# A decoder kernel on one core: table load, two preparations, one copy and six identity turns moved or cut in the sparse attention stage

## The chip, the core and the metric

The kernel runs on one core of a Trainium2 chip. A core has a matrix engine (TensorE, PE in the profile), a vector engine (VectorE, DVE), an activation engine (ScalarE, ACT), a general engine (GpSimd, POOL) and a queue engine (SyncE, SP). Each follows its own list of instructions, and they meet only at semaphores. The metric is the device time of one execution in microseconds (us), less is better.

## The reference, cut to what matters

The reference is a decoder of two layers over 8 sequences of 256 tokens, width 128. The first layer is a recurrent attention, a memory attention and a mixture of experts with one expert each token; the second a sparse attention, a cross attention and a mixture with two experts each token. The change is in the sparse attention only:

```
def _sparse_causal_mask(q_len, k_len):
    cols = np.arange(k_len)
    rows = np.arange(k_len)[:, None]
    strided = cols % STRIDE >= STRIDE - C          # STRIDE 128, C 8
    local = cols[None, :] // STRIDE == rows // STRIDE
    causal = cols[None, :] <= rows
    layout = (strided[None, :] | local) & causal
...
q, k, v = (split(q), split(k), split(v))           # 16 heads of 8
scores = jnp.einsum('bhqd,bhkd->bhqk', q, k) * scale
scores = jnp.where(mask, scores, mask_value)
attn = jax.nn.softmax(scores, axis=-1)
out = jnp.einsum('bhqk,bhkd->bhqd', attn, v)
out = out.transpose(0, 2, 1, 3).reshape(B, S, E)
return out @ W_proj + b_proj
```

A query in the first 128 tokens of a sequence sees the keys of its own tile of 128 up to itself. One in the second 128 sees, besides those, the last 8 keys of the first tile; these are called the far keys.

## The kernel before

The 8 sequences go through in 4 groups of 2, that is 512 tokens or 4 tiles of 128 each time. Every group passes the stages memory, first mixture, sparse attention, cross attention, second mixture, one after the other; the recurrent part of the next group is done beside the later stages. The order of work on each engine is written out by hand, and semaphores join the engines. ScalarE's program runs the first three groups as a loop and the last one after it.

In the sparse stage the scores of 16 heads are cut into 8 units. Unit u is eight heads of one tile (128 queries by 8 times 128 keys); the tiles go in the order 0, 1, 3, 2, two units each, so units 2 to 5 belong to tiles that have far keys. A unit passes these steps:

- `masked_scores(u)` on TensorE: the causal mask is laid into two PSUM banks (L868), and the scores are added (L880). From u = 2 on it waits for `s_arg`, since the banks of unit u - 2 must have been read.
- `unit(u)` on VectorE: the negative row maximum (L2113), for units with far keys its minimum with that of the far scores, `far_nmax` (L2116), then scores plus maximum into an SBUF buffer (L2120), which counts `s_arg` up.
- `exps(u)` on ScalarE: the exponential of that buffer (L1423), which counts `s_exp` up.
- `turn_probs(u)` on TensorE: 16 transposes into PSUM banks 4 and 5 (L893). It waits for `s_exp` and for `sT_ready`, that the turned probabilities of unit u - 1 were copied out of these banks.
- `turned(u)` on ScalarE: that copy (L1239, 128x1024), which counts `sT_ready` up.
- `values(n)` on TensorE for each tile, after both its units (L920, L925).

For the far keys there are apart from this a score for each sequence (L860), a copy of these scores by ScalarE (L1239, 128x256, which counts `far_ready` up), and on VectorE two preparations: `Vg`, the far values under the head mask (L2166), and `far_nmax` (L2170). `far_exps(b)` (L1437) is their exponential on ScalarE, `turn_far` (L900) their transpose.

An exponential and a Gelu are in different function tables of ScalarE. The first mixture ends with a Gelu, so a table is loaded ahead of the first exponential of the sparse stage. `keep_awake(5, n)` (L494) is n transposes of the identity into an unused part of bank 5; nobody reads the result. `decay_e` is a column of 128 that is read once, before the first group; the memory stage already computes it again at its start.

Of the kernel before, what the change touches and what calls it, by code (L numbers as in the profile page):

```python
# [9 lines left out]
ACT = mybir.ActivationFunctionType  # L10
# [30 lines left out]
R_LNG, R_LNB, R_FLNG, R_FLNB, R_DECAY, R_FIRST, R_MK, R_MV, R_MR, R_FMK, R_FMR, R_NORMW = range(12)  # L41
# [21 lines left out]
def decoder_kernel(  # L63
# [10 lines left out]
    with ExitStack() as stack:  # L74
        def sb(name, shape, dt=F32):
            return stack.enter_context(nc.sbuf_tensor(name, shape, dt))
# [27 lines left out]
        decay_e = sb("decay_e", [P, 1])  # L104
# [187 lines left out]
        def bank(i):  # L292
            return ps[:, i, :]

        def far_turn(n):
            return ps[:, 7, 2 * P:3 * P] if n == 1 else ps[:, 0, 0:P]
# [115 lines left out]
        def col(i):  # L412
            return cols[:, i:i + 1]
# [76 lines left out]
        def _(pe):  # L490
            def keep_awake(b, count):

                for _ in range(count):
                    pe.transpose(ps[:, b, 2 * P:3 * P], ident[:, :], ident[:, :])  # L494
# [343 lines left out]
            def sparse_attention(it):  # L838
# [45 lines left out]
                def turn_probs(u):  # L884
                    pe.wait_ge(s_exp, it * UNITS + u + 1)
                    if u:
                        pe.wait_ge(sT_ready, it * UNITS + u)
                    else:
                        pe.wait_ge(far_ready, it + 1)
                    for i in range(2 * QUAD):  # L890
                        for w in range(2):
                            r = slice(w * DK, (w + 1) * DK)
                            last = pe.transpose(ps[:, 4 + w, i * DK:(i + 1) * DK], SP_[u % 2][r, i, :], ident[r, r])  # L893
                    last.then_inc(sT_ps, 1)
# [43 lines left out]
                def masked_scores(u):  # L938
                    mask_scores(u)
                    scores(u)  # L940
# [2 lines left out]
                masked_scores(1)  # L943
                far_scores_of()
                masked_scores(2)
                keep_awake(5, 5)
                turn_probs(0)
                masked_scores(3)
                turn_probs(1)
# [272 lines left out]
            def group(it, more=True):  # L1222
                memory(it)
                mixture_top1(it)
                sparse_attention(it)
                cross_attention(it, more)
                mixture_top2(it, more)
# [9 lines left out]
        def _(act):  # L1237
            def copy(dst, src):
                return act.activation(dst, src, ACT.Copy)  # L1239
# [19 lines left out]
            def x_turned(it, n):  # L1259
                for seq in range(GROUP):  # L1260
                    act.wait_ge(xT_ps, (it * LAYERS + n - 1) * GROUP + seq + 1)
                    r = slice(seq * SEQ, (seq + 1) * SEQ)
                    copy(XT[:, r], ps[:, XT_BANKS[n - 1][seq], r]).then_inc(xT_ready, 1)
# [76 lines left out]
            def context_values(it, j, b, seq):  # L1340
                act.wait_ge(vx_ps, it * (2 * PAIRS) + V_ORDER.index((j, seq)) + 1)
                copy(values_of(j, seq), tiles(b)).then_inc(vx_ready, 1)
# [68 lines left out]
            def sparse_attention(it):  # L1411
                act.wait_ge(cols_ready, 6)
                x_turned(it, 3)
                context_values(it, 3, 6, 0)
                act.wait_ge(qkv_ps, it * 4 + 1)
                act.activation(qT[:, :], bank(1), ACT.Identity, bias=battq_scaled[:, 0:1], scale=float(HD) ** -0.5)\
                    .then_inc(qk_ready, 1)
                act.wait_ge(qkv_ps, it * 4 + 2)
                act.activation(kT[:, :], bank(2), ACT.Identity, bias=col(R_BATT + 1)).then_inc(qk_ready, 1)

                def exps(u):
                    act.wait_ge(s_arg, it * UNITS + u + 1)
                    act.activation(SP_[u % 2], SP_[u % 2], ACT.Exp).then_inc(s_exp, 1)  # L1423

                def turned(u):
                    act.wait_ge(sT_ps, it * UNITS + u + 1)
                    if u in (3, 4):
                        act.wait_ge(so_ps, it * TT + 1)
                    if u == 5:
                        act.wait_ge(s_ps, it * UNITS + UNITS)  # L1430
                    if u in (6, 7):
                        act.wait_ge(so_ps, it * TT + 2)
                    copy(sp_turned[u], ps[:, 4:6, :].rearrange("p b n -> p (b n)")).then_inc(sT_ready, 1)

                def far_exps(b):
                    act.wait_ge(g_arg, it * GROUP + b + 1)
                    act.activation(G[:, b, :], G[:, b, :], ACT.Exp).then_inc(g_exp, 1)  # L1437

                def far_turned(b):
                    act.wait_ge(gT_ps, it * GROUP + b + 1)  # L1440
                    copy(GT[:, b, :], far_turn(SP_ORDER.index(b * QT + 1))).then_inc(gT_ready, 1)

                act.wait_ge(far_ps, it + 1)
                copy(far_scores, ps[:, 4, 0:GROUP * P].rearrange("p (b n) -> p b n", b=GROUP)).then_inc(far_ready, 1)
                exps(0)
                turned(0)
                exps(1)
                turned(1)
                exps(2)
                exps(3)  # L1450
                far_exps(0)
                turned(2)
                exps(4)
                turned(3)
                far_turned(0)
                exps(5)
                far_exps(1)
                turned(4)
                turned(5)
                exps(6)  # L1460
                exps(7)
                turned(6)
                far_turned(1)
                turned(7)
                context_values(it, 2, 3, 1)
# [115 lines left out]
            def group(it, more=True):  # L1581
                memory(it)
                mixture_top1(it)
                sparse_attention(it)
                cross_attention(it, more)
                mixture_top2(it, more)
# [225 lines left out]
        def _(dve):  # L1812
# [293 lines left out]
            def sparse_attention(it):  # L2106
                def unit(u):
                    n, w = u // 2, u % 2
                    t = SP_ORDER[n]
                    nm = s_nmax[:, n, w * 2 * QUAD:(w + 1) * 2 * QUAD]  # L2110
                    scored = ps[:, 2 * w:2 * w + 2, :].rearrange("p b (i k) -> p (b i) k", k=P)
                    dve.wait_ge(s_ps, it * UNITS + u + 1)
                    dve.tensor_reduce(nm, scored, AX.X, ALU.max, negate=True)  # L2113
                    dve.drain()
                    if t % QT == 1:
                        dve.tensor_tensor(nm, nm, far_nmax[:, t // QT, w * 2 * QUAD:(w + 1) * 2 * QUAD], ALU.min)  # L2116
                        dve.drain()
                    if u >= 2:
                        dve.wait_ge(sT_ps, it * UNITS + u - 1)
                    dve.tensor_tensor(SP_[u % 2], scored, nm.unsqueeze(2).to_broadcast([P, 2 * QUAD, P]), ALU.add)\  # L2120
                        .then_inc(s_arg, 1)

                def far(n):
                    b = SP_ORDER[n] // QT
                    by_key = "p (h c) -> p h c"
                    dve.tensor_tensor(G[:, b, :].rearrange(by_key, c=CB), far_scores[:, b, :].rearrange(by_key, c=CB),
                                      s_nmax[:, n, :].unsqueeze(2).to_broadcast([P, NH, CB]), ALU.add).then_inc(g_arg, 1)
# [34 lines left out]
                                  bv_bc[:, :].unsqueeze(1).to_broadcast([P, GROUP, D]), ALU.add).then_inc(v_ready, 1)  # L2162
                for u in range(UNITS):
                    unit(u)
                    if u == 0:
                        dve.tensor_tensor(Vg.rearrange("p b (h d) -> p b h d", h=NH), Vgb,  # L2166
                                          head_mask[:, :].unsqueeze(2).unsqueeze(1).to_broadcast([P, GROUP, NH, HD]),
                                          ALU.mult)
                        dve.wait_ge(far_ready, it + 1)
                        dve.tensor_reduce(far_nmax[:, :, :], far_scores.rearrange("p b (h c) -> p b h c", c=CB), AX.X,  # L2170
                                          ALU.max, negate=True)
                    if u % 2 and SP_ORDER[u // 2] % QT == 1:
                        far(u // 2)
# [191 lines left out]
            def group(it, more=True):  # L2365
                memory(it)
                mixture_top1(it)
                sparse_attention(it)
                cross_attention(it, more)
                mixture_top2(it, more)  # L2370
# [39 lines left out]
```

## Time and profile before

| | us |
|---|---|
| median of 3 runs | 1101.97 |
| the runs | 1101.78 to 1103.04 |
| the profiled execution | 1103.46 |
| its span, first to last instruction | 1101.5 |
| TensorE busy | 1053.6 (96%) |
| VectorE busy | 724.1 (66%) |
| ScalarE busy | 643.1 (58%) |
| GpSimd busy | 167.1 (15%) |
| mean granted clock of TensorE | 0.998 |

The profile counts times from the first instruction of the span. TensorE's busy time is modelled at the ends of its matmuls, and a group of several matmuls is printed as one piece whose last end lies beyond the start of the next group. The four sparse stages begin near 122, 388, 653 and 918 us.

### The profile page before, as it was taken

The numbers are of one execution on the slowest core, as the hardware profiler recorded it, in microseconds if no ns is written. First come the engines' busy times: TensorE is split into PE (matmuls) and PEld (weight loads), VectorE is DVE, ScalarE is ACT, GpSimd is POOL, SyncE is SP. The second block draws the span as 40 slices with busy tenths as digits, with TensorE's granted clock in tenths as the row PEclk, the third lists the DMA queues.
The fourth block names the chain that finished last, engine by engine and source line by source line (L and its number), as shares of the span: only waits on it lengthen the run. The fifth ranks groups of instructions, "written<-read, shape, count | busy, mean of one in ns | idle before, by whom it ended". The sixth has DMA issues, their size and how long they took to land.

```text
span 1101.5 us, 23000 instructions
## 1 busy us (share of the span) xinstructions
PE 1053.6 (96%) x9039; PEld 666.0 (60%) x9039; DVE 724.1 (66%) x1841; ACT 643.1 (58%) x1428; POOL 167.1 (15%) x237
## 2 busy tenths in 40 slices
PE   7999999998999999999899999999999999999987
PEld 5663665556875556555687366555578646655567
DVE  6641767889653386888955158688975417677871
ACT  5550557776763266777566136777666505587724
POOL 3320400121020130111112022021212004000000
PEclk9999999999999999999999999999999999999999
DMA  8400000000000000000000000000000000000000
GB/s 254 140 1 1 1 2 11 14 9 1 1 11 1 1 1 2 11 21 1 2 2 10 1 1 2 11 1 21 2 1 10 1 1 1 2 1 1 2 2 10
DMA packets 21083, 15.74 MB, mean 14 GB/s; under 512 B 887, under 2 KB 18660, under 8 KB 20972
## 3 DMA queue, kind: packets, MB, share of 16 engines
q1 hardware_dynamic: 20948, 14.24, 4.3%
q8 instruction: 72, 1.18, 0.4%
q14 instruction: 39, 0.32, 0.1%
q10 hardware_dynamic: 24, 0.01, 0.0%
HBM read 13.18 MB, written 1.05 MB: 13 GB/s over the span
## 4 chain that ended last, share of the span: by engine, by line
PE 72%; DVE 11%; ACT 9%; issue 5%; DVEq 2%; POOL 1%; POOLq 0%; ACTq 0%; DMA 0%
PE ps L786 11%; PE ps L1020 8%; PE ps L984 8%; PE ps L1002 5%; PE ps L828 3%; PE ps L822 3%; PE ps L1172 3%; PE ps L1163 3%; PE ps L1029 2%; ACT arena L1476 2%; PE ps L819 2%; PE ps L920 2%; DVE nmax L2186 2%; ACT arena L1239 2%; PE ps L880 2%
## 5 line engine op out<-in xcount | busy, mean ns | idle before, releaser
L1239 ACT ACTIVATE arena<-ps 128x512 f32<-128x512 f32 (+7 forms) x296 | 159.6, 572 | 111.3 <-PE ps L1002 55.6
L2186 DVE TENSOR_REDUCE nmax<-ps 128x1 f32<-128x512 f32 x256 | 164.4, 684 | 23.6 <-PE ps L984 22.9
L1476 ACT ACTIVATE arena<-ps,nmax 128x512 f32<-128x512 f32 x256 | 173.8, 685 | 7.9 <-DVE nmax L2186 4.8
L1652 POOL TENSOR_TENSOR rstd<-mv,neg_half 128x2 f32<-128x2 f32 x72 | 49.9, 695 | 660.6 <-DVE mv L1826 660.5
L1002 PEld LDWEIGHTS ps<-ident,arena 64*128 64x128 f32 x2048 | 76.5, 138 | 79.0 <-issue 45.4
L2191 DVE COPY arena<-ps 128x512 f32<-128x512 f32 x128 | 88.2, 689 | 47.5 <-PE ps L1002 47.2
L786 PE MATMUL ps<-big,w1a 128*128 128x512 f32 x256 | 117.3, 604 | 0.1
L1002 PE MATMUL ps<-ident,arena 64*128 64x64 f32 x2048 | 92.6, 228 | 8.1 <-ACT arena L1239 2.7
L2078 DVE TENSOR_TENSOR big<-XT,ps 128x512 f32<-128x512 f32 x32 | 22.0, 688 | 90.7 <-PE ps L771 90.4
L786 PEld LDWEIGHTS ps<-big,w1a 128*128 128x128 f32 x256 | 46.3, 189 | 57.7 <-issue 56.5
L1401 ACT ACTIVATE big<-ps 128x512 f32<-128x512 f32 x16 | 9.6, 597 | 116.4 <-PE ps L786 116.4
L2195 DVE SCALAR_TENSOR_TENSOR X<-ps,cross_inv,X 128x128 f32<-128x128 f32 x240 | 68.5, 344 | 4.3 <-PE ps L1029 0.8
L828 PEld LDWEIGHTS ps<-xwT,ctxT 128*128 128x128 f32 x512 | 62.7, 192 | 11.0 <-issue 10.8
L828 PE MATMUL ps<-xwT,ctxT 128*128 128x128 f32 x512 | 65.4, 277 | 0.0
L822 PE MATMUL ps<-ctxT,xwT 128*128 128x512 f32 x128 | 62.8, 596 | 1.4 <-ACT ctxT L1239 1.4
L1476 ACT ACTIVATION_READ_ACCUMULATOR arena<-ps,nmax 128x1 f32 x256 | 51.7, 202 | 0.0
L1029 PEld LDWEIGHTS ps<-xwT,arena 64*128 64x128 f32 x480 | 30.5, 187 | 19.2 <-DVE arena L2191 15.1
L2120 DVE TENSOR_TENSOR arena<-ps,s_nmax 128x1024 f32<-128x1024 f32 x32 | 39.2, 1225 | 2.4
L2113 DVE TENSOR_REDUCE s_nmax<-ps 128x8 f32<-128x1024 f32 x32 | 39.0, 1217 | 2.6 <-PE ps L880 2.6
L1423 ACT ACTIVATE arena<-arena 128x1024 f32<-128x1024 f32 x32 | 33.6, 1054 | 7.6 <-DVE arena L2120 7.5
L1029 PE MATMUL ps<-xwT,arena 64*128 64x128 f32 x480 | 36.2, 284 | 1.9 <-ACT arena L1239 1.9
L1553 ACT ACTIVATE arena<-ps,cols 128x80 f32<-128x80 f32 x128 | 31.0, 329 | 10.3 <-PE ps L1163 10.3
(393 smaller groups left out, 2009.1 us busy)
## 6 DMA issues: line engine op xcount, KB each, us to landing
ctx<-in_ctx_dram SPq DMA_DIRECT2D x4, 512.0 KB, 4.0
w1a<-in_L_ffn_W_dram SPq DMA_DIRECT2D x1, 2048.0 KB, 9.5
w1b<-in_L_ffn_W_dram SPq DMA_DIRECT2D x1, 2048.0 KB, 11.6
w2b<-in_L_ffn_W_dram SPq DMA_DIRECT2D x8, 256.0 KB, 6.0
X<-in_x_dram SPq DMA_DIRECT2D x4, 256.0 KB, 2.8
out_dram<-Y SPq DMA_DIRECT2D x3, 256.0 KB, 2.3
arena<-in_L_xattn_Wq_dram SPq DMA_DIRECT2D x1, 512.0 KB
arena<-in_L_xattn_Wk_dram SPq DMA_DIRECT2D x1, 512.0 KB
```

The lines of the kernel that those rows point to most:

```text
L786: last = pe.matmul(bank(acc[h]), w1a[:, e, h * P:(h + 1) * P], XE[:, e % 2, :], start=(e == 0), stop=(e == E - 1))
L822: pe.matmul(bank(b), xwT[:, 1, j, :], ctxT[:, seq * CTX:(seq + 1) * CTX], start=True, stop=True)\
L828: last = pe.matmul(ps[:, b, k * P:(k + 1) * P], ctxT[:, c * P:(c + 1) * P], xwT[:, 2, j, :], start=True, stop=True)
L984: pe.matmul(bank(2 * (t % 2) + h), QTs[r, j % 2, t * P:(t + 1) * P], keys_of(j, t // QT)[r, :], start=True, stop=True).then_inc(c_ps, 1)
L1002: last = pe.transpose(ps[:, 4 + u, o:o + DK], cprob[r, 2 * (t % 2) + h, k * P:(k + 1) * P], ident[r, r])
L1020: last = pe.matmul(ps[r, 6, seq * SEQ:(seq + 1) * SEQ], values_of(j, seq)[:, k, r], cprobT[:, :, o:o + DK], start=(k == 0), stop=(k == KT ...
L1029: last = pe.matmul(ps[:, b + h, t * D:(t + 1) * D], CTs[r, j % 2, t * P:(t + 1) * P], xwT[r, 3, j, :], start=True, stop=True)
L1239: return act.activation(dst, src, ACT.Copy)
L1476: act.activation(cprob[:, 2 * (t % 2) + h, :], bank(2 * (t % 2) + h), ACT.Exp, bias=nmax[:, s:s + 1], accum_out=rsum[:, j % 2, s:s + 1]).t ...
L2186: dve.tensor_reduce(nmax[:, s:s + 1], bank(s % 4), AX.X, ALU.max, negate=True)\
L2191: dve.tensor_copy(cprobT[:, 2 * (t % 2), :], bank(4)).then_inc(cT_even, 1)
L2195: last = dve.scalar_tensor_tensor(out=X1[:, t, :], in0=ps[:, b, t * D:(t + 1) * D], scalar=cross_inv[:, j % 2, 2 * t + h:2 * t + h + 1], i ...
```

## The change

Four edits, all in the sparse stage:

- ScalarE computes `decay_e` once more, an exponential of one column, right behind the copy of the keys `kT`. The table load that stood ahead of `exps(0)` now stands ahead of this instruction.
- VectorE does `Vg` and `far_nmax` behind unit 1 instead of behind unit 0.
- ScalarE does `turned(4)` ahead of `far_exps(1)` instead of behind it.
- TensorE does 2 identity transposes instead of 5 ahead of `turn_probs(0)`.

```diff
@@ TensorE, sparse_attention
                 masked_scores(2)
-                keep_awake(5, 5)
+                keep_awake(5, 2)
                 turn_probs(0)
@@ ScalarE, sparse_attention
                 act.activation(kT[:, :], bank(2), ACT.Identity, bias=col(R_BATT + 1)).then_inc(qk_ready, 1)
+                act.activation(decay_e[:, :], col(R_DECAY), ACT.Exp)
...
                 exps(5)
+                turned(4)
                 far_exps(1)
-                turned(4)
                 turned(5)
@@ VectorE, sparse_attention
                 for u in range(UNITS):
                     unit(u)
-                    if u == 0:
+                    if u == 1:
                         dve.tensor_tensor(Vg.rearrange("p b (h d) -> p b h d", h=NH), Vgb,
...
                         dve.wait_ge(far_ready, it + 1)
                         dve.tensor_reduce(far_nmax[:, :, :], far_scores.rearrange("p b (h c) -> p b h c", c=CB), AX.X,
                                           ALU.max, negate=True)
```

ScalarE's list at the start of the stage, before, from the copies of the queries and keys to the second exponential (`o_max` is the buffer of the far scores, `arena` holds the units):

```order
L1416 ACTIVATE qT<-ps,battq_scaled 128x512 [waits qkv_ps]
L1419 ACTIVATE kT<-ps,cols 128x512 [waits qkv_ps]
L1239 ACTIVATE o_max<-ps 128x2x128 [waits far_ps]
L1422 ISA
L1423 ACT_TABLE_LOAD
L1423 ACTIVATE arena<-arena 128x1024 [waits s_arg]
L1239 ACTIVATE arena<-ps 128x1024 [waits sT_ps]
```

The same place of the changed kernel, whose lines on ScalarE are one further on from here:

```order
L1416 ACTIVATE qT<-ps,battq_scaled 128x512 [waits qkv_ps]
L1419 ACTIVATE kT<-ps,cols 128x512 [waits qkv_ps]
L1420 ACT_TABLE_LOAD
L1420 ACTIVATE decay_e<-cols 128x1
L1239 ACTIVATE o_max<-ps 128x2x128 [waits far_ps]
L1423 ISA
L1424 ACTIVATE arena<-arena 128x1024 [waits s_arg]
L1239 ACTIVATE arena<-ps 128x1024 [waits sT_ps]
```

The load has moved ahead of the wait for the far scores, with the short exponential behind it; the number of loads is the same.

VectorE's list from the first unit on, before (`ctx` is here the storage of `Vg`):

```order
L2113 TENSOR_REDUCE s_nmax<-ps 128x8
L2120 TENSOR_TENSOR arena<-ps,s_nmax 128x1024
L2166 TENSOR_TENSOR ctx<-ctx,head_mask 128x256
L2170 TENSOR_REDUCE far_nmax<-o_max 128x32
L2113 TENSOR_REDUCE s_nmax<-ps 128x8
L2120 TENSOR_TENSOR arena<-ps,s_nmax 128x1024
L2113 TENSOR_REDUCE s_nmax<-ps 128x8
L2116 TENSOR_TENSOR s_nmax<-s_nmax,far_nmax 128x8
```

And in the changed kernel, with the same instructions:

```order
L2114 TENSOR_REDUCE s_nmax<-ps 128x8
L2121 TENSOR_TENSOR arena<-ps,s_nmax 128x1024
L2114 TENSOR_REDUCE s_nmax<-ps 128x8
L2121 TENSOR_TENSOR arena<-ps,s_nmax 128x1024
L2167 TENSOR_TENSOR ctx<-ctx,head_mask 128x256
L2171 TENSOR_REDUCE far_nmax<-o_max 128x32
L2114 TENSOR_REDUCE s_nmax<-ps 128x8
L2117 TENSOR_TENSOR s_nmax<-s_nmax,far_nmax 128x8
```

The two preparations now stand between units 1 and 2.

ScalarE's list around unit 5, before (`q_den` is the copy of turned far probabilities, `p_num` the far exponential):

```order
L1239 ACTIVATE q_den<-ps 128x128 [waits gT_ps]
L1422 REGISTER_ALU
L1423 ACTIVATE arena<-arena 128x1024 [waits s_arg]
L1436 REGISTER_ALU
L1437 ACTIVATE p_num<-p_num 128x128 [waits g_arg]
L1239 ACTIVATE arena<-ps 128x1024 [waits so_ps,sT_ps]
```

And in the changed kernel:

```order
L1239 ACTIVATE q_den<-ps 128x128 [waits gT_ps]
L1423 REGISTER_ALU
L1424 ACTIVATE arena<-arena 128x1024 [waits s_arg]
L1239 ACTIVATE arena<-ps 128x1024 [waits so_ps,sT_ps]
L1437 REGISTER_ALU
L1438 ACTIVATE p_num<-p_num 128x128 [waits g_arg]
```

The copy of unit 4 and the far exponential have changed places.

## Rows read from the trace of the kernel before

**Rows 1.** The page: busy time of each engine

```profile
PE 1053.6 (96%) x9039; PEld 666.0 (60%) x9039; DVE 724.1 (66%) x1841; ACT 643.1 (58%) x1428; POOL 167.1 (15%) x237
```

**Rows 2.** Waits of TensorE, whole span: total us, times, longest us

```profile
PE ps L893 <- ACT arena L1239: 2.1, 4, 0.5
```

**Rows 3.** Timeline of TensorE, second group: start us, us, line, operation [idle before]

```profile
395.03 0.60 PE L868 MATMUL ps<-causal,ident_bf 128*128 128x512 bf16 x2 [0.39 <-DVE arena L2120]
...
396.62 0.77 PE L494 MATMUL ps<-ident 128*128 128x128 f32 x5
397.48 0.71 PE L893 MATMUL ps<-ident,arena 64*128 64x64 f32 x16
398.22 0.61 PE L868 MATMUL ps<-causal,ident_bf 128*128 128x512 bf16 x2
...
400.26 0.71 PE L893 MATMUL ps<-ident,arena 64*128 64x64 f32 x16 [0.38 <-ACT arena L1423]
400.99 0.60 PE L868 MATMUL ps<-causal,ident_bf 128*128 128x512 bf16 x2
...
409.10 0.71 PE L893 MATMUL ps<-ident,arena 64*128 64x64 f32 x16
409.74 0.60 PE L868 MATMUL ps<-causal,ident_bf 128*128 128x512 bf16 x2
...
411.93 0.71 PE L893 MATMUL ps<-ident,arena 64*128 64x64 f32 x16 [0.52 <-ACT arena L1239]
```

**Rows 4.** Timeline of VectorE, second group

```profile
393.75 1.22 DVE L2120 TENSOR_TENSOR arena<-ps,s_nmax 128x1024 f32<-128x1024 f32 x1
394.89 0.51 DVE L2166 TENSOR_TENSOR ctx<-ctx,head_mask 128x256 f32<-128x256 f32 x1
395.32 0.41 DVE L2170 TENSOR_REDUCE far_nmax<-o_max 128x32 f32<-128x256 f32 x1
395.65 1.21 DVE L2113 TENSOR_REDUCE s_nmax<-ps 128x8 f32<-128x1024 f32 x1
396.94 1.23 DVE L2120 TENSOR_TENSOR arena<-ps,s_nmax 128x1024 f32<-128x1024 f32 x1
398.08 1.22 DVE L2113 TENSOR_REDUCE s_nmax<-ps 128x8 f32<-128x1024 f32 x1
...
399.70 1.23 DVE L2120 TENSOR_TENSOR arena<-ps,s_nmax 128x1024 f32<-128x1024 f32 x1
```

**Rows 5.** Timeline of ScalarE, second group

```profile
394.67 0.39 ACT L1239 ACTIVATE o_max<-ps 128x256 f32<-128x256 f32 x1 [4.38 <-PE ps L860]
395.08 1.28 ACT L1423 ACT_TABLE_LOAD   x1
396.37 1.06 ACT L1423 ACTIVATE arena<-arena 128x1024 f32<-128x1024 f32 x1
...
399.16 1.05 ACT L1423 ACTIVATE arena<-arena 128x1024 f32<-128x1024 f32 x1
...
409.62 1.06 ACT L1423 ACTIVATE arena<-arena 128x1024 f32<-128x1024 f32 x1 [0.97 <-DVE arena L2120]
410.58 0.29 ACT L1437 ACTIVATE p_num<-p_num 128x128 f32<-128x128 f32 x1
410.78 1.00 ACT L1239 ACTIVATE arena<-ps 128x1024 f32<-128x1024 f32 x1
```

**Rows 6.** One line's instructions on VectorE: min/median/max ns, first and last start

```profile
L2116 DVE TENSOR_TENSOR s_nmax<-s_nmax,far_nmax x16: 166/168/261, 133.6 to 938.7; 128x8 f32<-128x8 f32 x16
```

**Rows 7.** TensorE by stretch: length, busy us (instructions), granted clock, DMA share, GB/s

```profile
3.40:6.80 3.40, 2.27 (x15) 1.00 0.39 82
6.80:12.00 5.20, 4.16 (x14) 0.67 0.82 243
397.60:401.00 3.40, 2.98 (x39) 1.00 0.03 7
794.00:797.40 3.40, 2.51 (x28) 1.00 0.00 0
```

## The prediction

> **What bounds the kernel now.** I read the page first. TensorE is busy for 96% of the span and no other engine above 66% [rows 1], so a gain must shorten a piece in which TensorE stands still, or take work from it. Then I read TensorE's waits over the whole span. The largest that lies in the sparse stage on a copy by ScalarE comes 4 times, once in each group, 2.1 us together [rows 2]. Last I laid the timelines of the three engines of one group side by side, from 393 to 412 us. The second group (388 to 424 us) stands for all four; the other groups show the same steps to some hundredths.
>
> The first units are a race between three engines, and the reader should look for who is never idle. It is VectorE. From the end of unit 0 on, its instructions follow each other without a gap: L2120 at 393.75, L2166 at 394.89, L2170 at 395.32, the maximum of unit 1 at 395.65, its subtraction at 396.94, the maximum of unit 2 at 398.08, its subtraction from 399.70 to 400.93 [rows 4]. None of these rows has a bracket of idle time. TensorE follows: it starts unit 2's mask at 395.03, after L2120 ended at 394.97; unit 3's at 398.22, after 398.17; unit 4's at 400.99, after 400.93 [rows 3, 4]. Each time 0.05 to 0.06 us lie between, so each of the three starts is set by VectorE's `s_arg`. TensorE's other stop here is 0.38 us ahead of `turn_probs(1)` at 400.26 [rows 3], for the exponential that ran from 399.16 to 400.21 [rows 5].
>
> From 400.99 on no row of TensorE carries idle time until unit 7's scores, whose mask starts at 409.74, are done; then it waits 0.52 us for `turned(4)` before `turn_probs(5)` at 411.93 [rows 3]. ScalarE's rows show why: `exps(5)` could start only at 409.62, when VectorE released it; the far exponential followed at 410.58, and the copy that TensorE wants at 410.78, ending at 411.78 [rows 5].
>
> **Table load.** Before, it takes 395.08 to 396.36, and the first exponential starts at 396.37 [rows 5]. Its argument was ready at 394.97 [rows 4] and the far copy ended at 395.06, so without the load the exponential starts at about 395.05, 1.32 us earlier, and ends at 396.1. In its new place the load costs nothing: ScalarE was idle for 4.38 us ahead of the far copy at 394.67 [rows 5], from 390.29 on, and load and a short exponential take 1.28 plus at most 0.3 us (the row of the 128x128 exponential, 0.29 [rows 5], which is larger). That leaves 2.8 us of cover. If that cover were gone, the load would be back where it was, and no worse.
>
> **Identity transposes.** Five of them take 0.77 us in one row, of which the last's tail is not spacing; `turn_probs(0)` came at 397.48, after the exponential ended at 397.43 [rows 3, 5]. They start at 396.62, when unit 2's scores have been issued. With the exponential done at 396.1, TensorE is what `turn_probs(0)` waits for, and two transposes put it at about 396.9 (0.77 times 2/5 gives 0.31 at most). So it starts 0.6 us earlier. Three fewer in each group is 3 times 0.77/5, 0.46 us; it counts only if no one else is waited for next.
>
> **The two preparations.** From start to start they take 0.43 and 0.33 us [rows 4], 0.76 together. Behind unit 1, they let its argument be ready 0.76 us earlier, at 397.41. Unit 2 is behind them in both orders: its maximum starts at 398.08 as before, and `s_arg` for it comes at 400.93 as before. That is the step on which the forecast turns. Following the new early path: `turn_probs(0)` 396.9, its copy about 397.65 to 398.67, `exps(1)` from 398.57 to 399.6, `turn_probs(1)` at about 399.67 instead of 400.26, finished by 400.4. And then unit 4's mask waits for `s_arg` until 400.99, where it stood before. Load, transposes and early unit 1 together buy 0.6 us of TensorE's time, and TensorE spends them in front of VectorE. Sum of these three edits: 0.0 us. VectorE has no less work than before in front of 400.93, and no wait of its own in it that could be shortened.
>
> Could the preparations cost more or less in the new place? GpSimd works beside them in both. The only row that shows such an operation at two prices is L2116: 166 ns at the least and 261 at the most [rows 6], 0.1 us between. I bound the two preparations and the L2116 behind them together by 0.1 us either way in each group, and take nothing, since they have company in both places. An increase would go straight into the end, as VectorE is the bound here: 0.4 us in all.
>
> **The copy ahead of the far exponential.** `turned(4)` may start as soon as `exps(5)` lets it; its input was ready, since `turn_probs(4)` was issued at 409.10 [rows 3]. It takes the place at 410.58 in place of 410.78 [rows 5], 0.20 us, and `turn_probs(5)` goes from 411.93 to 411.73. Its other condition, the exponential of unit 5, is met at 410.68. Of the 0.52 us wait 0.32 remain. The far exponential moves behind, to about 411.5, and ends by 411.8; its transpose comes on TensorE behind `turn_probs(6)`, later than 415, so it has over 3 us of cover. What follows on TensorE until the end of the stage has no stop except for VectorE's division, which itself starts from TensorE's values. So the 0.20 us are kept. Bounds: nothing, if ScalarE pays something at the turn, and 0.20 plus nothing above, since `exps(5)` is fixed by VectorE at 409.62.
>
> **The sum.** 4 groups times 0.20 us is 0.8 us; the bounds are 0.4 less for dearer preparations and a possible loss of the 0.8, or 0.4 more for cheaper ones. Against the profiled execution of 1103.46 us (span 1101.5) that is 1102.7. That execution was 1.5 us above the median of the runs, 1101.97, and a fixed difference is carried over, so 1101.2 us.
>
> **Rivals.** *The early path reaches the end* (faster). If unit 4's mask at 400.99 had been held by `turn_probs(1)` and not by VectorE, 0.6 us more would be gained in each group. For it: `turn_probs(1)` ended just there, 400.26 plus 0.71. Against it: elsewhere a mask follows 0.64 us behind the start of the turns (409.10 to 409.74), here 0.73 [rows 3], and VectorE's end at 400.93 does not move. It would give 4 times 0.8, 1098.8 us. Its extreme, that the whole 1.32 us of the load come off in each group beside the 0.20, gives 4 times 1.52, 1095.9. It decides only if VectorE can start unit 2 earlier than 398.08. 8 in 100 for both, of which 3 for the extreme.
>
> *Nothing at all.* The 0.20 us are lost in a dearer start of the copy or in dearer preparations: 1102.0, 14 in 100.
>
> *The clock falls* (slower). TensorE is given fewer idle-filling transposes, and its stops grow from 0.1 and 0.38 us to about 0.47 and 0.6. In the stretch from 397.6 to 401.0 it was busy for 2.98 of 3.4 us [rows 7]; by the times above, unit 3's scores until 399.2 and the turns of 0.71, it would be 2.3. At the start of the kernel a stretch with 2.27 of 3.4 was followed by one in which the granted clock was 0.67 of 2.4 GHz: with two levels, 3.4 of its 5.2 us at 1.2 GHz [rows 7], which costs half, 1.7 us of TensorE's work. Four times that, less the 0.8, is 1108.0 us. Against it: a stretch with 2.51 busy kept 1.00 in the middle of the kernel [rows 7], and here the stretches ahead and behind are full. The fall must be triggered in the one short stretch after unit 2. 5 in 100.
>
> The Trainium skill (TensorE: Matmul & The Clock Gate, section "A second HAM failure mode: psum-queue depth-cycling") says that many small idles of TensorE between groups of matmuls can make its clock swing between the two levels, and that throughput is lost to it. By that rule this rival would be what happens. The trace of this kernel has such small idles in every stage and a granted clock of 1.00 around them, which does not agree.
>
> **How the numbers follow.** The forecast has 73 in 100, with its own range 1100.6 to 1101.9. With nothing at all (14), the two kinds of the early path (8) and the clock (5), that is 100. Repeated runs of before spread over 1.3 us, so the range of 8 in 10 is 1100.2 to 1102.6, which takes in forecast and nothing-at-all with that spread. About 0.2%, 2.2 us, is what a measurement can tell from no change. Forecast and nothing-at-all are inside it; the early path is beyond it on the one side, the clock on the other. Faster 0.10, same 0.84, slower 0.06.
>
> **What the profile would show.** Right: the first exponential of the stage at once behind the far copy; `turn_probs(0)` about 0.6 us earlier; `turn_probs(1)` 0.6 earlier; a new wait of TensorE for L2120's successor, about 0.6 us, ahead of unit 4's mask, once a group; unit 4's mask at the same distance from the stage's start; the 2.1 us of waits for ScalarE's copy down to 1.3. Wrong: unit 4's mask closer to the start of the stage (early path), a longer time of the preparations (nothing), or a granted clock below 1.00 in any stretch of a sparse stage (clock).

## The result, and the profile after

The changed kernel takes 1116.41 us in the median (1113.09 to 1119.06, 4 runs) against 1101.88 (1101.74 to 1103.04, 4 runs) for the kernel before: a ratio of 1.0124, interval 1.0104 to 1.0144 (the ratios here are taken over all runs and are not exactly the quotients of the medians). By the medians that is 14.5 us slower, where 0.8 us faster was forecast. The profiled execution, the longest of the four, took 1119.06 us, its span 1117.0.

The timeline of TensorE in the second group of the changed kernel (start us, us, line; idle time ahead in brackets) answers to [rows 3]. Its stage starts 3.65 us later than in before, so 3.65 is to be taken off for a comparison:

```profile
398.68 0.60 PE L868 MATMUL ps<-causal,ident_bf 128*128 128x512 bf16 x2 [0.39 <-DVE arena L2121]
399.22 1.13 PE L880 MATMUL ps<-arena,qT 32*128 32x512 f32 x4
400.28 0.44 PE L494 MATMUL ps<-ident 128*128 128x128 f32 x2
400.64 0.71 PE L893 MATMUL ps<-ident,arena 64*128 64x64 f32 x16
401.29 0.61 PE L868 MATMUL ps<-causal,ident_bf 128*128 128x512 bf16 x2
...
403.42 0.71 PE L893 MATMUL ps<-ident,arena 64*128 64x64 f32 x16 [0.47 <-ACT arena L1424]
405.62 1.03 PE L868 MATMUL ps<-causal,ident_bf 128*128 128x512 bf16 x2 [1.49 <-DVE arena L2121]
406.58 2.08 PE L880 MATMUL ps<-arena,qT 32*128 32x512 f32 x4
...
419.40 0.71 PE L893 MATMUL ps<-ident,arena 64*128 64x64 f32 x16 [0.33 <-ACT arena L1239]
```

`turn_probs(0)` comes at 396.99 in the time of before (forecast 396.9), `turn_probs(1)` at 399.77 (forecast 399.67), the wait for `turned(4)` is 0.33 us (forecast 0.32). But unit 4's mask (L868 at 405.62) is at 401.97 in the time of before, where it stood at 400.99: TensorE stood still for 1.49 us, where a stop of about 0.6 was forecast. And that mask takes 1.03 us, the scores behind it 2.08 where the same four matmuls took 1.13 at 399.22. The engine runs at half speed there. The stretches of the same trace say so (length, busy us, granted clock):

```profile
398.70:404.10 5.40, 4.93 (x46) 1.00 0.00 0
404.10:405.30 1.20, 0.03 (x2) 0.96 0.05 14
405.30:412.10 6.80, 6.48 (x70) 0.50 0.00 1
412.10:425.00 12.90, 12.49 (x205) 1.00 0.00 1
```

In this group the clock falls to 1.2 GHz at the end of the long stop, just ahead of the mask, and rises again 6.8 us later. The groups are not alike in this, though the stop is 1.48 or 1.49 us in all four. In the third and fourth the low stretch is as long and begins while the mask runs. In the first, mask and scores still run at full speed and the low stretch is half as long: the granted clock is 0.79 from 137.0 to 140.4 and 0.71 from 140.4 to 143.8 us, which with two levels makes 3.4 us at the lower one. The timeline of VectorE, which answers to [rows 4], shows why the stop is long:

```profile
399.83 1.22 DVE L2121 TENSOR_TENSOR arena<-ps,s_nmax 128x1024 f32<-128x1024 f32 x1
400.97 1.14 DVE L2167 TENSOR_TENSOR ctx<-ctx,head_mask 128x256 f32<-128x256 f32 x1
402.04 0.41 DVE L2171 TENSOR_REDUCE far_nmax<-o_max 128x32 f32<-128x256 f32 x1
402.37 1.21 DVE L2114 TENSOR_REDUCE s_nmax<-ps 128x8 f32<-128x1024 f32 x1
403.65 0.62 DVE L2117 TENSOR_TENSOR s_nmax<-s_nmax,far_nmax 128x8 f32<-128x8 f32 x1
404.34 1.22 DVE L2121 TENSOR_TENSOR arena<-ps,s_nmax 128x1024 f32<-128x1024 f32 x1
```

The masking of `Vg` (L2167) takes 1.14 us where it took 0.51, the small minimum behind the row maximum (L2117) 0.62 where it took 0.26. Unit 2's argument is ready at 405.56, that is 401.91 in the time of before, 0.98 us late. VectorE is never idle in these rows; what it lost stands inside the durations. Both slow operations read two tensors from SBUF; the subtraction (L2121), which takes one of its two from PSUM, keeps its 1.22 us beside GpSimd's work. GpSimd's timeline of the same trace shows what runs beside them:

```profile
400.80 1.04 POOL L1748 TENSOR_TENSOR arena<-kT,quad_mask 128x512 f32<-128x512 f32 x1
401.79 1.45 POOL L1770 TENSOR_TENSOR NHAT<-X,row_bc 128x512 f32<-128x512 f32 x1
403.20 1.04 POOL L1748 TENSOR_TENSOR arena<-kT,quad_mask 128x512 f32<-128x512 f32 x1
```

The masking starts 0.17 us after a key tile product (L1748) and ends at 402.11, 0.3 us after that product made way for the next. The minimum starts at 403.65 inside the second product, the last of these rows, and ends at 404.27, 0.03 us after it.

The last view is the distance from the first mask (L868) of one sparse stage to that of the next, read off the timelines. It is free of what differs from run to run before the first stage:

| kernel | first mask of stages 1 to 4, us | distances | less before |
|---|---|---|---|
| before | 124.94, 390.75, 656.00, 921.35 | 265.81, 265.25, 265.35 | |
| changed | 126.12, 394.40, 663.50, 932.86 | 268.28, 269.10, 269.36 | 2.47, 3.85, 4.01 |

### The profile page after: what moved, and what is told of

Its sections match the earlier page's. It is cut to its first block, busy times and chain, and to the rows that moved or that the text cites. A ratio compares the mean times of both kernels' runs of the same rounds, so it can differ in the third digit from the quotient of the medians.

```text
span 1117.0 us, 22980 instructions
## 1 busy us (share of the span) xinstructions
PE 1064.6 (95%) x9027; PEld 673.1 (60%) x9027; DVE 728.3 (65%) x1841; ACT 644.3 (58%) x1432; POOL 166.7 (15%) x237
## 4 chain that ended last, share of the span: by engine, by line
PE 71%; DVE 13%; ACT 7%; issue 4%; DVEq 3%; POOL 1%; ACTq 0%; POOLq 0%; DMA 0%
PE ps L786 10%; PE ps L1020 8%; PE ps L984 8%; PE ps L1002 5%; PE ps L828 3%; PE ps L822 3%; PE ps L920 3%; PE ps L1172 3%; PE ps L1163 3%; PE ps L1029 2%; ACT arena L1477 2%; PE ps L819 2%; DVE nmax L2187 2%; DVE arena L2121 2%; ACT arena L1239 1%
## 5 line engine op out<-in xcount | busy, mean ns | idle before, releaser
L2121 DVE TENSOR_TENSOR arena<-ps,s_nmax 128x1024 f32<-128x1024 f32 x32 | 39.2, 1225 | 12.6 <-PE ps L893 10.5
L880 PE MATMUL ps<-arena,qT 32*128 32x512 f32 x128 | 38.9, 686 | 0.0
```

## The experiments

Where distances between the sparse stages are given, the three numbers are those of the profiled execution against those of before in the table above.

**Each edit apart.** Two theories stood against each other: that the moved preparations meet GpSimd ("port", later "lock"), and that the cut from five identity transposes to two lets the clock fall ("transposes").

`a1_prep_only`, the kernel before with one edit:

```diff
-                    if u == 0:
+                    if u == 1:
                         dve.tensor_tensor(Vg.rearrange("p b (h d) -> p b h d", h=NH), Vgb,
...
```

> Only the two preparations of VectorE are moved behind unit 1; load, copy order and five transposes stay as before. Theory 'port': the masking of Vg meets a GpSimd tile product in its new place and takes about 1.14 us in place of 0.51, and the small minimum behind it up to 0.6 in place of 0.26, so unit 2's argument comes 0.6 to 1.0 us late in each group and TensorE's stop ahead of unit 4's mask is about 0.6 to 1.0 us. Time at least 1104.5 (clock kept) and up to 1116 (clock falls). Rival 'transposes' (the cut from five to two let the clock fall): granted clock as before, time 1102 to 1106, and no row of the masking above 0.6 us is needed.

Measured: 1117.55 us against 1102.14, ratio 1.0123 (1.0094 to 1.0153); distances 2.89, 4.31 and 4.38 us more. This edit alone brings the whole loss, with five transposes in place. TensorE's stop ahead of unit 4's mask is 1.33 us and the mask 1.31 us late, more than the 0.6 to 1.0 expected, since the minimum took 0.94 us and not 0.6 at most: it began earlier in GpSimd's product (401.78 to 402.82 in this trace) and ended at 402.85, again 0.03 us after it. VectorE's two lines, of its timeline:

```profile
399.22 1.15 DVE L2166 TENSOR_TENSOR ctx<-ctx,head_mask 128x256 f32<-128x256 f32 x1
...
401.91 0.94 DVE L2116 TENSOR_TENSOR s_nmax<-s_nmax,far_nmax 128x8 f32<-128x8 f32 x1
```

`a2_no_prep`, the changed kernel with the preparations back behind unit 0:

```diff
-                    if u == 1:
+                    if u == 0:
```

> Everything of the change but the moved preparations: early load, copy ahead of the far exponential, two transposes. Theory 'port': masking of Vg stays at 0.51 us, unit 4's mask stands where it stood in before, granted clock 0.998, time 1101.1 (0.8 less than before). Rival 'transposes': the clock falls in the sparse stages all the same, 1107 to 1117.

Measured: 1102.01 us against 1102.14, ratio 0.9996 (0.9987 to 1.0006), by the time alone no change that can be told; granted clock 1.00 in all sparse stages; distances 0.19, 0.21 and 0.14 us less. Masking 0.51 us. Load, transposes and copy harm nothing, and of the three only the copy's 0.2 us arrives: `turn_probs(0)` and `turn_probs(1)` come 0.49 and 0.45 us earlier, unit 4's mask stands 10.22 us behind the stage's first mask, where it was 10.24, with a stop of 0.46 us ahead of it.

`a3_five_turns`, the changed kernel with the transposes as before:

```diff
-                keep_awake(5, 2)
+                keep_awake(5, 5)
```

> The changed kernel with five identity transposes again. Theory 'port': masking still 1.14 us, TensorE's stop ahead of unit 4's mask still over 1.2 us, clock still falls, 1109 to 1118. Rival 'transposes': clock back to 0.998, 1101 to 1106.

Measured: 1116.52 us against 1102.14, ratio 1.0091 (1.0060 to 1.0122); distances 2.66, 3.93 and 4.10 us more, masking 1.15 us, a stop of 1.33 us. The theory "transposes" is out. Two of its five runs, of 1107.72 and 1109.20 us, had a granted clock of 0.997 and 0.996, the other three 0.987 or 0.988.

`a4_copy_only`, the kernel before with `turned(4)` ahead of `far_exps(1)`:

```diff
-                far_exps(1)
                 turned(4)
+                far_exps(1)
```

> Only the copy of unit 4 ahead of the far exponential. Both theories: the wait of TensorE for that copy falls from 0.52 to 0.32 us in each group, 0.8 us less in all: 1101.1, ratio 0.9993.

Measured: 1102.55 us against 1102.14, ratio 0.9997 (0.9988 to 1.0006). Its time alone can't be told from no change. The waits of TensorE for the copy over the whole span, which answers to [rows 2]:

```profile
PE ps L893 <- ACT arena L1239: 1.3, 4, 0.3
```

2.1 us became 1.3, the 0.8 of the forecast; of it 0.20, 0.08 and 0.13 us stand in the distances.

**What makes the masking dear.** `b1_swap`, the changed kernel with the order of the two preparations turned round:

```diff
                     if u == 1:
-                        dve.tensor_tensor(Vg.rearrange("p b (h d) -> p b h d", h=NH), Vgb,
...
                         dve.wait_ge(far_ready, it + 1)
                         dve.tensor_reduce(far_nmax[:, :, :], far_scores.rearrange("p b (h c) -> p b h c", c=CB), AX.X,
...
+                        dve.tensor_tensor(Vg.rearrange("p b (h d) -> p b h d", h=NH), Vgb,
...
```

> The changed kernel with the far maximum ahead of the masking of Vg behind unit 1. Theory 'lock' (a VectorE operation with two inputs in SBUF stands until the GpSimd operation that runs beside it has ended): the masking starts 0.33 us later, against the same GpSimd tile product, and ends where it did, so its row shrinks from 1.14 to about 0.8 us; the small minimum then comes earlier and waits longer for the next GpSimd product, about 0.95 in place of 0.62 us; unit 4's mask does not come earlier, time 1110 to 1119. Rival 'dear beside GpSimd' (a fixed price of company): masking 1.14 again, minimum 0.62 again, the same place of the mask, so the two rows tell them apart.

Measured: 1116.08 us against 1103.28, ratio 1.0122 (1.0108 to 1.0137), distances 2.37, 4.00 and 3.89 us more. VectorE's timeline, then GpSimd's:

```profile
397.98 0.41 DVE L2168 TENSOR_REDUCE far_nmax<-o_max 128x32 f32<-128x256 f32 x1
398.31 0.81 DVE L2170 TENSOR_TENSOR ctx<-ctx,head_mask 128x256 f32<-128x256 f32 x1
399.04 1.21 DVE L2114 TENSOR_REDUCE s_nmax<-ps 128x8 f32<-128x1024 f32 x1
400.33 0.95 DVE L2117 TENSOR_TENSOR s_nmax<-s_nmax,far_nmax 128x8 f32<-128x8 f32 x1
```

```profile
397.80 1.04 POOL L1748 TENSOR_TENSOR arena<-kT,quad_mask 128x512 f32<-128x512 f32 x1
398.80 1.47 POOL L1770 TENSOR_TENSOR NHAT<-X,row_bc 128x512 f32<-128x512 f32 x1
400.21 1.05 POOL L1748 TENSOR_TENSOR arena<-kT,quad_mask 128x512 f32<-128x512 f32 x1
```

0.81 and 0.95 us, as the lock theory had them (0.8 and 0.95), where a fixed price would have left 1.14 and 0.62. The masking starts 0.34 us later against the same product and ends at the same place, 0.32 us after the next GpSimd row has begun: it waits for the product's end and then does about its own work (0.41 us when alone, by `d2_gpsimd_away` below). The far maximum, a reduction with one input from SBUF, takes its 0.41 us beside the same product.

`d2_gpsimd_away`, the changed kernel with all of VectorE, ScalarE and TensorE as it is, and GpSimd's second key tile and sum later:

```diff
@@ GpSimd, group
-                pool.wait_ge(s_ps, it * UNITS + 2)
+                pool.wait_ge(s_ps, it * UNITS + 4)
                 keys_of_tile(2)
-                pool.tensor_tensor(NHAT[:, :, :], X[:, :, :], bproj_bc[:, :].unsqueeze(1).to_broadcast([P, TT, D]),
-                                   ALU.add).then_inc(base_ready, 1)
                 pool.wait_ge(s_ps, it * UNITS + 4)
                 keys_of_tile(3)
+                pool.tensor_tensor(NHAT[:, :, :], X[:, :, :], bproj_bc[:, :].unsqueeze(1).to_broadcast([P, TT, D]),
+                                   ALU.add).then_inc(base_ready, 1)
```

> The changed kernel, VectorE, ScalarE and TensorE as in it; only GpSimd's second key tile waits until unit 3's scores are done and its sum for the projection comes last, so that nothing of GpSimd runs beside the masking of Vg and hardly anything beside the small minimum of unit 2. Lock theory: masking 0.42 us, minimum under 0.3, TensorE's stop ahead of unit 4's mask about 0.6 us in place of 1.49, clock 1.00, and so what the prediction said of the changed kernel: 0.8 us under before, ratio 0.9993; a group lasts 0.15 to 0.25 us less than in before. Rival (the place of the masking, or two inputs in SBUF, is dear by itself): masking 1.14 us and 1110 to 1118.

Measured: 1101.22 us (11 runs) against 1103.21 (18 runs), ratio 0.9987 (0.9978 to 0.9996); distances 0.21, 0.25 and 0.22 us less, granted clock 1.00. Of VectorE's timeline:

```profile
395.57 0.41 DVE L2167 TENSOR_TENSOR ctx<-ctx,head_mask 128x256 f32<-128x256 f32 x1
...
397.52 0.17 DVE L2117 TENSOR_TENSOR s_nmax<-s_nmax,far_nmax 128x8 f32<-128x8 f32 x1
```

With GpSimd away, the masking in its new place costs 0.41 us, the loss is gone, and the kernel's time is what the prediction gave the changed one, 0.2 us a group faster. So GpSimd's company is shown as the cause of the late argument. Its steps are not quite those of the prediction: masking and minimum are both cheaper than in before, unit 4's mask stands 10.04 us behind the stage's first where it was 10.24, and the stop ahead of it is 0.32 us and not 0.6. Hardly anything of this second 0.2 us arrives at the next group; where it goes is not shown.

**What makes a late argument cost 15 us.** `b2_fill`, the changed kernel with transposes of the identity in the stop:

```diff
                 turn_probs(1)
+                pe.wait_ge(v_ready, it + 1)
+                keep_awake(7, 12)
                 masked_scores(4)
```

> The changed kernel with 12 identity transposes (about 1.5 us) into an unused bank ahead of unit 4's mask, where TensorE stood still for 1.49 us. VectorE is as late as in the changed kernel. Theory 'stop' (the long stop lets the clock fall, and most of the loss is the clock's): granted clock about 1.00 in the sparse stages, masking still 1.14 us, time 1102.1 plus 4 times (0.99 later argument less 0.20) = 1105.3. Rival 'lateness alone' (the loss is the late argument and what follows from it): 1112 to 1118 as the changed kernel.

Measured: 1106.53 us against 1103.28, ratio 1.0028 (1.0015 to 1.0041), which is 3.3 us; distances 0.79, 0.79 and 0.81 us more. VectorE is as late as in the changed kernel (masking 1.14 us), but the stretches of this trace read, from unit 2's mask on, with the filled stop as the second:

```profile
394.30:399.70 5.40, 4.93 (x47) 1.00 0.01 3
399.70:401.20 1.50, 1.49 (x14) 1.00 0.02 5
401.20:408.00 6.80, 6.79 (x111) 1.00 0.01 2
```

So the late argument itself is 0.80 us a group (0.99 late less 0.20 of the copy), 3.2 us in all, and the clock is the rest: 1.7, 3.1 and 3.2 us in the first three groups by the distances, and 1.0124 less 1.0028 or 10.6 us of the whole. A second reading takes in the fourth group: from unit 4's mask to unit 5's, the piece that holds the low stretch, the changed kernel takes 5.78, 7.16, 7.29 and 7.19 us, and `b2_fill`, like before, 4.12. That is 10.9 us in all.

`c1_double_reduce`, the kernel before with unit 2's row maximum computed twice:

```diff
+                    if u == 2:
+                        dve.tensor_reduce(nm, scored, AX.X, ALU.max, negate=True)
+                        dve.drain()
                     dve.tensor_reduce(nm, scored, AX.X, ALU.max, negate=True)
```

> The kernel before with unit 2's row maximum computed twice, and nothing else changed: unit 2's argument comes about 1.3 us late, with GpSimd's part as in before and masking at 0.51 us. Theory 'stop': TensorE stands about 1.3 us ahead of unit 4's mask and the clock falls as in the changed kernel, 1109 to 1118. Rival 'only 1.3 us each': 1102.1 plus 4 times 1.3 = 1107.3 at a granted clock of 0.998.

Measured: 1116.61 us in the median (1112.36 to 1117.88), ratio 1.0125 (1.0110 to 1.0140). In the profiled execution the distances are 2.34, 1.41 and 2.79 us more. Its second group stood 1.57 us ahead of unit 4's mask and kept its clock, its fourth 1.42 us and lost it:

```profile
403.20:410.00 6.80, 6.80 (x111) 1.00 0.00 0
```

```profile
923.00:955.00 32.00, 29.17 (x305) 0.89 0.01 2
```

The 1.41 us is what the lateness alone costs; with the clock lost it is 2.34 and 2.79. So a late argument that has nothing to do with GpSimd does the harm too, and a stop of this length may or may not cost the clock. That fits the spread of the times of the kernels that lose the clock (6.0 us for the changed one, 10.6 for `a3_five_turns`), against 3.3 at most for before. What decides whether a stop costs the clock is not shown.

**Two versions that keep the early path.** `b3_vg_late` is the changed kernel with only the far maximum behind unit 1:

```diff
                     if u == 1:
-                        dve.tensor_tensor(Vg.rearrange("p b (h d) -> p b h d", h=NH), Vgb,
...
                         dve.wait_ge(far_ready, it + 1)
                         dve.tensor_reduce(far_nmax[:, :, :], far_scores.rearrange("p b (h c) -> p b h c", c=CB), AX.X,
...
+                    if u == 4:
+                        dve.tensor_tensor(Vg.rearrange("p b (h d) -> p b h d", h=NH), Vgb,
...
```

> The changed kernel with the masking of Vg behind unit 4, where GpSimd has nothing to do and VectorE waits 0.35 us for scores; the far maximum, with one input, stays behind unit 1. Lock theory: masking 0.43 us, no stop above 0.5 us ahead of unit 4's mask, granted clock 1.00, unit 2's argument about 0.3 us earlier than in before (0.43 less masking, up to 0.2 more for the small minimum against GpSimd), with the 0.20 of the copy about 0.5 us a group: 1100.1, ratio 0.998. Rival (any early path lets the clock fall): 1108 or more.

Measured: 1102.25 us against 1103.28, ratio 0.9993 (0.9985 to 1.0002); distances 0.41, 0.14 and 0.35 us less, masking 0.42 us. The time alone can't be told from no change. By the distances the sign is as expected, the size about 0.3 us a group in place of 0.5; the small minimum of unit 2 still took 0.51 us beside GpSimd's sum. `d1_late_base` takes that away too, with GpSimd's sum behind `keys_of_tile(3)`, as in the diff of `d2_gpsimd_away` but without the changed wait:

> The changed kernel with the masking behind unit 4 and GpSimd's sum for the projection behind its third key tile. Lock theory: the small minimum of unit 2 falls from 0.51 to 0.17 us, unit 4's mask comes another 0.3 us earlier than with the masking behind unit 4 alone, TensorE's stop ahead of it is gone; a group lasts 0.5 to 0.8 us less than in before, ratio about 0.9975. Rival (VectorE is not the bound there any more): no earlier mask, a group 0.3 us less, ratio 0.999.

Measured: 1099.94 us (8 runs) against 1103.21, ratio 0.9971 (0.9960 to 0.9981); distances 0.69, 0.45 and 0.67 us less. It beats both kernels. TensorE's timeline has no wait ahead of unit 4's mask any more:

```profile
397.43 0.71 PE L893 MATMUL ps<-ident,arena 64*128 64x64 f32 x16 [0.47 <-ACT arena L1424]
398.12 0.61 PE L868 MATMUL ps<-causal,ident_bf 128*128 128x512 bf16 x2
```

That mask is 5.43 us behind unit 2's (392.69 in this trace), where it was 5.96 in before [rows 3].

## Why the prediction was wrong

- **VectorE as the bound of the first units: right.** In the changed kernel unit 4's mask follows the end of unit 2's subtraction by 0.06 us (405.56 to 405.62), as in before, and every kernel in which that argument came earlier or later moved the mask with it. In `d1_late_base` two things come together: the argument is ready at 398.06, and the turns that began at 397.43 are done by the mask at 398.12. Those turns had waited 0.47 us for ScalarE's exponential, so there VectorE is no longer the bound alone.
- **Load and identity transposes: right.** Load in ScalarE's idle time, 0.0 us in the sum; `turn_probs(0)` and `turn_probs(1)` 0.5 us earlier (forecast 0.6) and spent in front of VectorE. `a2_no_prep` shows it.
- **Copy ahead of the far exponential: right in the wait** (0.52 to 0.33 us), and in the distances 0.1 to 0.2 us a group.
- **The two preparations: this step failed.** The prediction said: "I bound the two preparations and the L2116 behind them together by 0.1 us either way in each group, and take nothing, since they have company in both places." The term was 0.99 us a group (0.63 for the masking, 0.36 for the minimum), ten times the bound. What was wrong was to take company as a constant. What counts is who starts first and how much of the other's instruction is left. In before, the masking began at 394.89 [rows 4], when a GpSimd product had about 0.2 us to go, as GpSimd's timeline of before has it:

```profile
394.05 1.08 POOL L1763 TENSOR_TENSOR Y<-V,quad_heads 128x512 f32<-128x512 f32 x1
395.08 1.25 POOL L1763 TENSOR_TENSOR O<-V,quad_heads 128x512 f32<-128x512 f32 x1
```

  It cost 0.1 us over the 0.41 that `d2_gpsimd_away` shows; in the new place, a product had just begun. The row of L2116 with its two prices, 166 and 261 ns [rows 6], was the same lock caught near its end, and I read it as the size of the effect. In before the minimum of unit 2 ends 0.03 us after GpSimd's sum (VectorE's row, then GpSimd's):

```profile
399.37 0.26 DVE L2116 TENSOR_TENSOR s_nmax<-s_nmax,far_nmax 128x8 f32<-128x8 f32 x1
398.33 1.27 POOL L1769 TENSOR_TENSOR NHAT<-X,row_bc 128x512 f32<-128x512 f32 x1
```

  GpSimd's rows beside the new place were not laid out, though they could have been.
- **The Trainium skill had the rule**, on SBUF — State Buffer, section "Who interferes with whom": a VectorE instruction with two inputs in SBUF contends with a GpSimd instruction that reads SBUF, and the order of issue decides which of them stands until the other is through; a reduction does not contend. The traces here agree: 0.81 and 0.95 us in `b1_swap`, the reduction at 0.41 throughout. It was not weighed in the prediction.
- **The rival of the clock: right in kind and place, wrong in its cause, chance and price.** It put the fall down to the fewer identity transposes; `a3_five_turns` has the fall with all five, `a2_no_prep` keeps the clock with two. It was given 5 in 100, since the stop was reckoned at 0.6 us; with 1.49 us the clock is most of the loss. Its price was 1.7 us a fall, from the start of the kernel. That is what the fall cost in the first group (1.7 us); in the other three the low stretch is twice as long, 6.8 us, and costs 3.0 to 3.2 us, since all of what runs in it is TensorE's work. Without the late argument (`a2_no_prep`, `d2_gpsimd_away`) the stops of about 0.5 us that were forecast did not cost the clock in a profiled stage.
- **The sum.** Forecast -0.8 us; measured +14.5: -0.8 for the copy, +4.0 for 4 arguments 0.99 us late, which `b2_fill` measures together as +3.3; the other 11 are the clock's, 10.6 by the ratios of the two kernels and 10.9 by the pieces behind unit 4's mask. The changed kernel's profiled execution had one more fall of the clock, between 24 and 30 us (granted clock 0.72 there, 1.00 in before), ahead of the first sparse stage, where all the edits lie; what that has to do with the change stays open.

## What to carry to other kernels

Before an operation of VectorE with two inputs in SBUF is moved, lay GpSimd's timeline beside its new place: in this kernel it cost up to its own time plus what was left of GpSimd's instruction, and the profile showed that as a longer instruction, not as a wait. On the engine that everyone waits for, put such operations where GpSimd is idle, or move GpSimd's work, as `d1_late_base` does for 3 us. And price a delay ahead of TensorE twice, as lateness and as a possible fall of the clock: here 1 us of lateness in a group cost 2.5 us in the first group and 4 in the next two, with the copy's 0.2 us already taken off.

## What was not expected of the hardware

A minimum on 128x8 elements, 0.17 us when alone, took up to 0.95 us beside GpSimd. The fall of TensorE's clock is not a fixed reaction to a stop: in one execution of `c1_double_reduce` a stop of 1.57 us kept the clock and one of 1.42 us lost it. In the second group of the changed kernel it stayed at 1.2 GHz for 6.8 us, though TensorE was busy for 6.48 of them; in the first group, after a stop of the same length, it was low for half of that.
